# Masked cross-attention: the value products of a pair of heads issued as one block, and the softmax sums spread by 32-column tiles

## The reference, cut to what matters

```python
qh, kh, vh = heads(q @ Wq.T), heads(ctx @ Wk.T), heads(ctx @ Wv.T)   # 16 heads, d = 32
scores = einsum('bhqd,bhkd->bhqk', qh, kh)                           # 128 x 2048 per head
scores = where(mask, -1e9, scores) / sqrt(32)
attn = softmax(scores)
out = einsum('bhqk,bhkd->bhqd', attn, vh)
x = x + merge(out) @ Wo.T
```

## Time and profile before

| | |
|---|---|
| median of three runs | 1761.82 us (1760.24 to 1762.29) |
| the profiled execution | 1760.35 us, of which 1758.9 us are the span of the core's instructions |
| TensorE busy | 1684.7 us (96%), 11102 matmuls |
| VectorE busy | 1070.8 us (61%) |
| ScalarE busy | 908.5 us (52%) |
| masked cross-attention | from about 656 us to 1271 us of the span |

### The profile page before, as it was taken

One profiled execution on the slowest core, in us unless ns is written; L12 is line 12 of the kernel. 1 busy time (PEld: TensorE's weight loads), 2 busy tenths in 40 slices (PEclk: granted clock), 3 DMA queues, 4 the chain that ended last, 5 costly groups with the idle time before them and its releaser, 6 DMA issues.

```text
span 1758.9 us, 29329 instructions
## 1 busy us (share of the span) xinstructions
PE 1684.7 (96%) x11102; PEld 1274.4 (72%) x11102; DVE 1070.8 (61%) x2282; ACT 908.5 (52%) x1910; POOL 126.1 (7%) x75
## 2 busy tenths in 40 slices
PE   7999999998999999999999999999999987999998
PEld 5778888886878788777777777756545555777776
DVE  5777777774643325555555555588744435787865
ACT  6666667562154224444444454477623334676763
POOL 0000000000000011000100010000011102223213
PEclk9999999998999999999999999999999997999999
DMA  6332323214620399777867786778760033888852
GB/s 234 116 108 84 96 85 96 85 60 174 239 96 0 114 287 323 228 236 216 238 190 232 220 239 185 209 197 227 256 242 7 7 132 124 285 307 288 285 194 75
DMA packets 147259, 308.53 MB, mean 175 GB/s; under 512 B 11453, under 2 KB 101565, under 8 KB 135549
## 3 DMA queue, kind: packets, MB, share of 16 engines
q1 hardware_dynamic: 145564, 301.65, 53.4%
q0 software_dynamic: 1536, 4.76, 0.9%
HBM read 225.16 MB, written 81.22 MB: 174 GB/s over the span
## 4 chain that ended last, share of the span: by engine, by line
PE 86%; DVE 5%; ACT 4%; issue 2%; DMA 1%; DVEq 1%; SPq 0%; POOL 0%; ACTq 0%; POOLq 0%
PE bank L128 16%; PE bank L130 14%; PE bank L129 14%; PE bank L1299 7%; PE bank L1321 5%; PE bank L1675 4%; PE bank L1289 3%; PE bank L2199 3%; PE bank L2203 2%; PE bank L2200 2%; PE bank L2234 2%; PE bank L1768 2%; PE bank L1332 2%; ACT T L1818 1%; DVE WS L2514 1%
## 5 line engine op out<-in xcount | busy, mean ns | idle before, releaser
L1418 DVE CUSTOM_DVE_ANT_0 TT<-bank,MASK 128x512 f32<-128x512 f32 x256 | 174.7, 683 | 22.5 <-PE bank L1289 21.8
L1365 ACT ACTIVATE TT<-TT,MX 128x512 f32<-128x512 f32 x256 | 183.5, 722 | 0.2
L2514 DVE TENSOR_TENSOR WS<-EW,WS 128x1024 fp32r<-128x1024 f32 (+1 forms) x120 | 146.9, 1234 | 59.2 <-ACT WS L2345 58.2
L2345 ACT CAST WS<-EW 128x1024 fp32r<-128x1024 f32 (+1 forms) x144 | 139.1, 977 | 50.4 <-PE bank L2203 48.7
L1299 PE MATMUL bank<-IDN,TT 128*128 128x128 f32 x1024 | 159.9, 279 | 0.0
L128 PE MATMUL bank<-BCH,WKT 128*128 128x256 f32 x512 | 154.6, 302 | 4.3 <-DVE BCL L355 4.3
L1431 DVE COPY PT<-bank 128x512 f32<-128x512 f32 x128 | 88.3, 690 | 102.1 <-PE bank L1299 99.3
L130 PE MATMUL bank<-BCH,WKT 128*128 128x256 f32 x512 | 145.3, 284 | 0.0
L129 PE MATMUL bank<-BCL,WKT 128*128 128x256 f32 x512 | 145.1, 283 | 0.0
L1299 PEld LDWEIGHTS bank<-IDN,TT 128*128 128x128 f32 x1024 | 116.0, 140 | 33.0 <-issue 22.2
L1373 ACT COPY PT<-bank 128x512 f32<-128x512 f32 x128 | 75.3, 588 | 113.1 <-PE bank L1299 113.0
(11 more groups left out here) (333 smaller groups left out, 3831.3 us busy)
## 6 DMA issues: line engine op xcount, KB each, us to landing
EW<-in_ewg SPq DMA_DIRECT2D x48, 1024.0 KB, 6.1
KST<-tmp_k SPq DMA_DIRECT2D x43, 768.0 KB, 5.7
tmp_k<-EKH SPq DMA_DIRECT2D x128, 256.0 KB, 2.8
EW<-in_ewg SPq DMA_DIRECT2D x24, 768.0 KB, 4.4
CT<-in_ctxT SPq DMA_DIRECT2D x32, 512.0 KB, 3.5
CN<-in_ctxN SPq DMA_DIRECT2D x32, 512.0 KB, 3.5
BCT<-in_ctxT SPq DMA_DIRECT2D x32, 512.0 KB, 4.4
tmp_k<-EKL SPq DMA_DIRECT2D x64, 256.0 KB, 2.8
```

The costliest lines, as they stand in the source:

```text
L1365: act.activation(TT[:, n % 4, cs], TT[:, n % 4, cs], ACT.Exp, bias=MX[:, n % 4, 5:6], scale=SC1, accum_out=SUM[:, b % 2, h, kc:kc + 1]).th ...
L1418: dve.tensor_tensor_reduce(TT[:, sl, 512 * kc:512 * kc + 512], bank[(0, 1, 4)[g % 3]][:], MASK[:, b % 2, 512 * kc:512 * kc + 512], 1.0, NE ...
L2345: act.copy(WS[:, i % NR, 0, 0:n * w], EW[q % NE][:, at:at + n * w]).then_inc(*w_high.up)
L2514: dve.tensor_tensor(WS[:, i % NR, 1, 0:n * w], EW[q % NE][:, at:at + n * w], f(WS[:, i % NR, 0, 0:n * w]), ALU.subtract).then_inc(*w_low.up)
```

## The change

All eight value products of a pair are issued one after another, in the step in which the last of them was issued before (`g % 8 == 1`, from `g` = 9 on). For that `PT` gets twelve slots instead of four. The sums are spread by four matmuls with 32 columns of weights each instead of two with 64; they stand at the head of the block. The lists of the other engines stay as they are, but for the copies into `PT`, which wait for `value(g - 12)` instead of `value(g - 4)`.

```diff
-        NP = 4
+        NP, NV = 12, 8
         PT = A("PT", [128, NP, 512])
...
                     pe.wait_ge(*sums_diag[p])
-                    for h in range(2):
-                        m = pe.matmul(bank[vb][64 * h:64 * h + 64, 256:384], ONES[:, 0:64], DG[:, h, :], start=True,
+                    for row in range(0, 128, 32):
+                        m = pe.matmul(bank[vb][row:row + 32, 256:384], ONES[:, 0:32], DG[:, row // 64, :], start=True,
                                       stop=True)
                     m.then_inc(*sums_mm.up)
...
                     if g % 8 == 2:
                         bg2(1)
-                    value(g - 2)
+                    if (g - 2) % NV == NV - 1:
+                        for v in range(g - 1 - NV, g - 1):
+                            value(v)
                 if g % 8 != 2:
                     bg2(1)
```

## The result

The kernel after takes 1700.82 us in the median of four runs (1699.55 to 1701.85), the kernel before 1761.62 us in four runs beside them. The ratio is 0.9656, with a 95% interval of 0.9639 to 0.9672: 3.4% faster. The forecast was 1698 us, within 1688 to 1712. The profiled execution took 1701.79 us, of which 1700.5 us are its span.

A forecast was written before the change was run, and what follows sets the result against it. TensorE's list was taken as the bound with background work, VectorE as the coming bound without it; gains of 49.6 + 11.8 + 2 = 63.4 us off the profiled 1760.35 us gave 1697.0, a median of 1698 us, range 1688 to 1712.

The forecast's parts named there:

- The fixed price of a chain: On TensorE each `value` carries 0.33 us independent of its number of products, to be paid once a pair instead of eight times.
- The chain's pace: In the block, each four matmuls in column tiles take 0.109 us on TensorE, as in the expert stage.
- Part 1: Pairs with background work, TensorE the bound: 2.48 us saved in each of 20 pairs, 49.6 us.
- The wait in `pair_sums`: VectorE waits for the sums, about 1 us in pairs with background work: costed at nothing, at most 0.25 us a pair.
- Part 2: Pairs without background work: VectorE becomes the bound, 10.66 us falls to 9.4 us a pair, 11.8 us gained.
- the tie at the sums: Without background work, VectorE's `DG` product comes about when the sums are done: 0 to 0.1 us of wait.
- the cost of the transfers: Transfer engines' busy share goes from 0.74 to 0.83 with background work: no cost taken, up to 3 us in the range.
- Part 3: End of the stage, from the last scores to the last value product: no change, within 2 us either way.
- The block on top of VectorE's list in part 2: Rival: VectorE and ScalarE run dry during the block; pairs up to 11.5 us, 1706 to 1718 us; chance 0.12.
- VectorE no bound: Rival: VectorE's time without background work is mostly short waits for TensorE; pairs of 8.3 us, 1688 us; chance 0.05.
- The block exposed in every pair: Rival: TensorE waits for VectorE and ScalarE after the block in all 31 pairs, 1770 us; chance 0.03.
- The clock: Rival: TensorE's new short waits without background work bring its clock to 1.2 GHz; 16.6 us a pair, 1766 us; chance 0.04.

The follow-up runs named there:

- e2: The kernel before with only the sums changed to four matmuls of 32 columns, value products still one by one: 1756.67 us, ratio 0.9983.
- e3: The kernel after with blocks of four value products, two blocks a pair, and eight slots: 1709.63 us, ratio 0.9721.
- e1: The kernel after with the sums spread by the old two matmuls of 64 columns: 1704.31 us, ratio 0.969.
- e7: The kernel after with `pair_sums` four steps later on VectorE: 1703.45 us, ratio 0.9662.
- e6: The kernel after with the next stage's weight loads held back until the last key load is issued: 1697.52 us, ratio 0.9621.

## Why the prediction was right

**The fixed price of a chain.** It was worked out as 0.33 us from three places of a step. The step from e2 to the kernel after gives 0.33 us for each chain saved, e3 0.37 us for one chain more. The chain's pace was taken from the expert stage; the block needs 2.10 us, as forecast. The Trainium skill, page "TensorEngine Tiling (Array Packing)", section "Tiling Modes", states that changing the tiling mode drains TensorE while changing the tile doesn't; the trace agrees in so far as 0.10 us is paid before and 0.23 us in and behind each chain, and no such price between the tiles inside it (0.109 us for each four). The page gives no price.

**Part 1** was forecast as 2.48 us a pair and 49.6 us. The terms as printed give 3.3 + 0.87 - 1.75 = 2.42 us, not 2.45; the measured value lies between this and 2.48. It measured 21.39 - 18.93 = 2.46 us, and 50.4 us over steps 0 to 160. The wait in `pair_sums` showed, and longer than I had said. The waits in the first stretch after, in us in total, times, longest:

```profile
DVE YT L1442 <- PE bank L1314: 43.6, 19, 3.1
```

That is 2.3 us each where I had said about 1. It cost nothing: TensorE was busy for all of the stretch.

**Part 2** was forecast with pairs of 9.4 us and VectorE as the bound. They are 9.40, but VectorE's list sets only one half of a pair. The other half, 4.70 us, is set by the chain of copy, transposes, scores, block, transposes and scores (e1, e7). The hand-made timeline had this chain and held: the tie at the sums cost 0.18 us (0 to 0.1 forecast), the masking behind the block came 0.36 us later than before (0.2 forecast), and the multiplication didn't wait. The last step to 9.4 us was not worked out: 9.36 + 0.3 is 9.66, and what was taken off for short gaps had no row behind it. With the measured 0.36 us of new waits it comes to 9.36 + 0.36 - 9.40, some 0.3 us by estimate, so that the pair is right to 0.01 us is partly luck. The gain that I gave this part, 11.8 us, was reached only in e6: 10.7 us in steps 168 to 240 and 1.4 us behind them. The kernel after has 9.9 and lost 4.0 again.

**Where it was off.** The term that was mis-sized is the cost of the transfers. I had taken none, with up to 3 us in the range, and had worked from the mean share of 0.74 in part 1 (0.83 expected there, 0.82 measured). The place was part 2, where the next stage's weights are loaded between the keys at a fixed number of steps: pairs that are 12% shorter bring both closer together, the share rises to 1.02, and the load of 768 KB for the last head takes 14.65 us. By the table this costs 0.8 + 5.4 = 6.2 us, twice what the range had for it. 4 us of it are the wait, and some are slower matmuls behind it: the granted clock was 0.57 in the four microseconds after the wait (1192 to 1196), near the lower level of 1.2 GHz, and 1.00 in the next four. The gains of part 1 that were larger by 0.8 us than forecast, and 0.9 us more behind step 255, nearly cancel. Of the forecast 63.4 us the spans show 58.4, 5 us less. The median missed the forecast by only 2.4 us, because it lies 1.0 us below the profiled execution and not 1.5 us above it: that part is luck.

**Part 3** was taken as no change. Without the late keys (e6) the last steps before step 255 give 1.4 us, and what follows loses 0.9.

**The rivals.** The block on top of VectorE's list in part 2 didn't come: half of it would have meant 10.4 us a pair. It is on the path of half of each pair, but VectorE has most of its work to do beside it; in e7, where `pair_sums` isn't beside it, a pair takes 10.07 us. VectorE no bound would have meant 8.3 us a pair, and fell as well: it is busy for 95% of part 2. The block exposed in every pair didn't come either: TensorE is busy throughout part 1. The clock stayed at 1.00 in part 2 with TensorE's pauses, 0.37 us a pair instead of the 1.1 us forecast and 0.70 us at the longest; it stayed there in e7 too, with a pause of 0.83 us in each pair. It fell only after the wait of 4 us. The Trainium skill, page "TensorE: Matmul & The Clock Gate", section "A second HAM failure mode: psum-queue depth-cycling", names short idle times as a cause of a falling clock; no run here shows that for pauses of these lengths.

## What to carry to other kernels

Look at the start of the next group, not at the shown duration: going from the whole array to a chain in column tiles and back cost 0.33 to 0.37 us here beyond the products themselves, so eight short chains are worth collecting into one if their inputs can be kept that long. A block that holds one engine for 2.10 us cost only 0.36 us of new waits in a pair, since VectorE had independent work at that place in its list; moving such work out of the way of a short wait cost more (0.67 us a pair) than the wait (0.18 us). When a stage gets shorter, check the loads that were spaced by its steps: here they took back some 6 us of the gain.

## What the runs showed of the hardware that was not expected

Four float32 matmul instructions with 128 x 64 weights in two tiles took 0.15 us more ahead of a chain of 128 x 32 tiles than eight in the chain's own shape (e1, e2). That this is the price of going from one column tiling to another is one reading; it isn't shown. And a pause of 3.97 us in TensorE's work was followed by four microseconds at a granted clock of 0.57 (the 64 matmul instructions of the block are shown with 2.35 us instead of 1.93), while pauses of 0.83 us in every pair left it at 1.00 (e7). A load of 768 KB took 14.65 us to land among loads of 512 KB, and 5.75 us without them (e6).
